# A two-layer graph network on one core: a direct tile's five products stand two picks behind its own pick on TensorE, and not one

## The reference

```
h = relu(layernorm(x));  x = x + segment_sum((h * cj)[src], dst) * ci
h = relu(layernorm(x));  x = x + (1 + eps) * h + segment_sum(relu(h[src] + edge_attr), dst)
```

## Time and profile before

| | |
|---|---|
| time, median of 3 runs | 4798.12 us (4794.34 to 4802.32) |
| the profiled execution | 4791.23 us, span 4789.2 us |
| layer 0's batches (first to last pick row L1157) | 200.74 to 3004.58 us of the span |
| PE busy | 3721.2 us (78%) |
| DVE busy | 3812.7 us (80%) |
| ACT busy | 3261.3 us (68%) |
| POOL busy | 3497.5 us (73%) |
| PE waited for ACT at L1259 (products) | 68.2 us |
| ACT waited for PE at L987 (copies) | 426.3 us |

### The profile page before, as it was taken

One profiled execution on the slowest core, in us unless ns is written; L12 is line 12 of the kernel. 1 busy time (PEld: TensorE's weight loads), 2 busy tenths in 40 slices (PEclk: granted clock), 3 DMA queues, 4 the chain that ended last, 5 costly groups with the idle time before them and its releaser, 6 DMA issues.

```text
span 4789.2 us, 130194 instructions
## 1 busy us (share of the span) xinstructions
PE 3721.2 (78%) x43852; PEld 2888.9 (60%) x43852; DVE 3812.7 (80%) x11454; ACT 3261.3 (68%) x9090; POOL 3497.5 (73%) x3590
## 2 busy tenths in 40 slices
PE   0388888888888888888888899467767777777775
PEld 0266666666666666666666666356666666666664
DVE  9788888888888888888888886767777776777775
ACT  1377777777777777777777777456666766666664
POOL 6757777777777777777777777477777777777774
PEclk9999999999999999999999999778888888888887
DMA  6322222222222222222222221211212221211221
GB/s 111 63 51 54 57 54 54 54 56 54 54 54 56 54 53 54 56 54 53 54 56 54 53 54 44 72 39 54 57 43 54 57 57 54 58 49 48 57 57 26
DMA packets 439702, 262.77 MB, mean 55 GB/s; under 512 B 334660, under 2 KB 423732, under 8 KB 432632
## 3 DMA queue, kind: packets, MB, share of 16 engines
q1 hardware_dynamic: 322488, 187.55, 16.7%
q0 software_dynamic: 110816, 60.69, 6.7%
q10 hardware_dynamic: 5728, 5.82, 0.5%
HBM read 172.96 MB, written 80.85 MB: 53 GB/s over the span
## 4 chain that ended last, share of the span: by engine, by line
PE 32%; POOL 23%; DVE 19%; issue 13%; ACT 10%; DMA 2%; DVEq 1%; ACTq 0%; SPq 0%; POOLq 0%
POOL stage L759 22%; PE candidates L1247 18%; PE plain_ps L1259 7%; DVE arena L1753 7%; ACT message L987 5%; DVE arena L1729 4%; ACT centered L956 2%; PE sorted_agg L1187 2%; PE candidates L1157 1%; ACT arena L880 1%; POOL message L759 1%; PE key_rows L1230 1%; DMA stage<-in_edge_attr 1%; DVE counts L1475 1%; PE key_rows L1139 1%
## 5 line engine op out<-in xcount | busy, mean ns | idle before, releaser
L771 POOL DMA_INDIRECT records<-stage,place_i x1875 | 1879.0, 1002 | 696.2 <-issue 652.0
L759 POOL DMA_INDIRECT stage<-table,src_plain x1250 | 1246.9, 997 | 409.1 <-issue 377.3
L987 ACT ACTIVATE message<-candidates,member_is 128x96 bf16<-128x96 f32 x4560 | 1170.7, 377 | 429.4 <-PE candidates L1247 426.3
L1753 DVE TENSOR_SCALAR arena<-window_iota,dst_rel 128x224 bf16<-128x224 f16 (+1 forms) x4800 | 1091.2, 302 | 37.8
L880 ACT ACTIVATE arena<-key_rows 125x640 f16<-125x640 f16 x1000 | 653.2, 716 | 215.1 <-DVE arena L1729 83.2
L1187 PE MATMUL sorted_agg<-arena 128*96 128x224 bf16 (+1 forms) x5000 | 654.1, 285 | 161.0 <-DVE arena L1753 109.6
L1259 PE MATMUL plain_ps<-summed,message 128*96 128x224 bf16 x4560 | 609.2, 269 | 68.2 <-ACT message L987 68.2
L1187 PEld LDWEIGHTS sorted_agg<-arena 128*96 128x96 bf16 x5000 | 543.7, 137 | 186.1 <-issue 118.6
L1259 PEld LDWEIGHTS plain_ps<-summed,message 128*96 128x96 bf16 x4560 | 490.7, 128 | 269.6 <-ACT message L987 127.4
L1729 DVE TENSOR_SCALAR arena<-arena,row_key 125x1280 bf16<-125x1280 f16 x1000 | 554.7, 555 | 96.5 <-ACT arena L880 64.6
L1139 PE MATMUL key_rows<-ident,record 128*125 128x128 f16 x5000 | 425.8, 235 | 239.2 <-DMA record<-records 96.2
(11 more groups left out here) (228 smaller groups left out, 5139.0 us busy)
## 6 DMA issues: line engine op xcount, KB each, us to landing
record<-records SPq DMA_DIRECT2D x50, 1650.0 KB
stage<-in_edge_attr SPq DMA_DIRECT2D x125, 400.0 KB, 3.2
records<-pad SPq DMA_DIRECT2D x25, 1650.0 KB, 11.9
records<-stage,place_i POOLq DMA_INDIRECT x1875
stage<-table,src_plain POOLq DMA_INDIRECT x1250
message<-table,mid_src POOLq DMA_INDIRECT x288
xs<-in_x SPq DMA_DIRECT2D x8, 390.6 KB
table<-parts ACTq DMA_DIRECT2D x4, 585.9 KB
```

The source lines that it names most:

```text
L759: pool.indirect_dma_start(message[:, k, j, :] if l == 0 else rows[:, k, j, :], None, table0 if l == 0 else table1, bass.IndirectOffsetOnAx ...
L771: pool.indirect_dma_start(records, bass.IndirectOffsetOnAxis(ap=place_i[:, h, e:e + 1], axis=0), stage[:, h, e, :], None).then_inc(scatter ...
L987: last = nc.scalar.activation(direct_message[n % DB][:, m * WIDE:(m + 1) * WIDE], candidates[n % 2][:, m * WIDE:(m + 1) * WIDE], ACT.Copy, ...
L1753: last = nc.vector.tensor_scalar(dst_onehot(g, t), window_iota[:, 0:WA if tile == 0 else WT], dst_rel[:, h, tile:tile + 1], None, ALU.is_e ...
```

## The change

In the loop over the direct tiles, the products of tile n - 2 stand behind the pick of tile n, where those of tile n - 1 stood. The range moves with them, so that tiles 0 to 33 are still done in the loop and tiles 34 to 37 behind it.

```
-                            if 1 <= n <= DIRECTS - LATE:
-                                direct_products(b, n - 1)
+                            if 2 <= n <= DIRECTS - LATE + 1:
+                                direct_products(b, n - 2)
```

## The result

| | time, median | ratio to before, 95% interval |
|---|---|---|
| before, 5 runs beside those of after | 4802.32 us (4794.34 to 4806.27) | |
| after, 5 runs | 4820.59 us (4815.02 to 4825.13) | 1.0036 [1.0025, 1.0047] |

The change makes the kernel 0.36% slower, 18.3 us between the medians; the interval of the ratio is 12 to 23 us. The forecast was 4818, 19.8 us of it for the change. The profiled execution took 4815.02 us, its span is 4812.9. Layer 0 ends 16.3 us later than in the profile of before (the first gather of layer 1 stood at 3112.2 and stands at 3128.5). The two spans differ by 23.7 us; the other 7.4 lie in layer 1, where nothing was changed. From its first gather on, layer 1 takes 1677 to 1695 us in the fourteen profiles of this case, and before's is the shortest, so these 7.4 us are a spread of executions and not the change's.

A forecast was written before the change was run, and what follows sets the result against it. ScalarE bounds seven direct tiles, then TensorE; VectorE's ranking runs full. Terms 1.05 + 1.62 + 14.58 + 2.58 give 19.8 us, on the median 4798.1: 4818 us; likeliest 4809 to 4822, 8-in-10 range 4794 to 4832.

The forecast's parts named there:

- The waits for ScalarE: First direct tiles: TensorE's waits for ScalarE's copies move to picks, sum staying near 68 us; TensorE's path 0.
- The first rival: First direct tiles: TensorE's 68.2 us of waits for ScalarE go, kernel takes 4730 us; chance 0.04.
- The one-hot of tile 27: VectorE, step 5: it waits for products of tile 16 and starts 1.62 us later in batches 1 to 21.
- From DVE to the pick: Batch end: 1.62 us reaches the pick in full in six batches VectorE ends, 1.29 in 15 ScalarE ends.
- The second rival: VectorE's lateness is hidden before the next batch's one-hots: up to 5 us faster, 4793 us; chance 0.17.
- Odd batches: Stops behind odd batches' products, tied to SyncE's fill, shrink 1.0 to 1.3 us; a pair costs 1.62, nine pairs 14.58.
- the third rival: Odd batches' stops don't shrink, all lateness is passed on: 30.1 us, 4828 us; chance 0.17, with or without the clock.
- TensorE's clock: The 20 products in five fast batches might slow by 1.54 us each, 7.7 in all; taken as 0, 4 in range.
- batch 22: Near the end, VectorE's 1.54 us wait for a later pick takes nearly all the lateness: 0.
- batch 0: First batch, where VectorE had no such wait for products of tile 16 before: 1.05 us later.
- batches 20 and 21: Last pair counted, without a stop behind the odd batch's products: 2.58 us later together.
- the gain from the earlier picks: Direct phase: picks up to 35 end 0.48 us earlier; worth 0.33 us in 15 batches, at most 5.0 us.

The follow-up runs named there:

- the run of the early tiles: Kernel before, with only the products of the first tiles, where TensorE waits for ScalarE, moved back a pick: 4797.77 us, ratio 1.0004.
- the late rank by itself: Kernel before, order and ring kept, with two more VectorE operations at the head of each batch's ranking: 4825.24 us, ratio 1.0042.
- with the fill moved: SyncE's fill issued only once the next batch's keys are turned: 4791.36 us in before's order, 4813.04 in the changed; with 13 ring places 4785.04 and 4771.67.
- before's order with 10 places: Kernel before, order of products kept, with 10 places in the ring of direct one-hots instead of 11: 4837.58 us, ratio 1.0077.
- With 13 places: Ring of direct one-hots given 13 places instead of 11: changed order 4792.16 us (0.9977 of before), before's order 4803.42 us (1.0005).

## Why the prediction was right, step by step

**The waits for ScalarE.** Forecast: they keep about their sum and stand before picks. They did (74.9 us, 144), and ACT's copies of tiles 6 and 7 stood at the same distance to 0.06 us. The first rival falls with the run of the early tiles: waits moved, time the same.

**The one-hot of tile 27.** +1.62 us was forecast. In batch 11 the products of tile 16 start 1.65 us later, and the one-hot with them (39.67 us behind the phase's start, 38.02 before). The sum of DVE's waits was put at some 60 us and is 73.0: besides tile 27's, each of batches 1 to 21 has the wait of tile 26, which I named and did not size in full.

**From DVE to the pick.** The rank was forecast at 78.3 and is at 77.9 to 78.6 in batches 1 to 21 (79.8 to 80.3 in batches 2, 6, 10, 14 and 18, whose rank came late before, too), 1.48 us later in the mean where 1.62 was forecast; the pick's wait was forecast at 3.7 us for DVE in all batches, and is 3.68 to 5.89, for DVE, in batches 0 to 21. POOL's scatter in batch 10 began 81.30 us behind the phase's start and 79.66 before. The second rival, lateness hidden, falls with this and with the late rank by itself.

**Odd batches.** The forecast was 1.62 for a pair and it is 1.40 in the profile, nearer than two profiles can tell. The stops did shrink, by 12.2 us together, 1.35 each; 1.0 to 1.3 was forecast. But the reason was half of the truth. One sign that I had named failed: the stops end 13.1 to 14.6 us behind the fill and not 12.3 to 13.5, so their end no longer hangs on the fill alone. A stop is TensorE's branch back to the loop's start, which I hadn't looked for; the fill lengthens it, and with the fill moved it keeps 3.3 to 4.0 us. Here the stops had just enough above that floor, which is luck: nothing in the prediction said how far they could shrink. With a little more lateness they can't, and before's order with 10 places, expected at 26 us, cost 36. On the Trainium skill, "Runtime: NRT & Kernel Launch", section "Instruction fetch mechanics": its "mostly hidden" is said of crossing from one block of instructions to the next. These nine stops are taken branches, and of those the same section says that a target outside the current two pages has to be fetched before execution can go on. The traces agree with that: 3.3 to 7.8 us with a transfer of instructions in each of the nine, and 0.08 us in batch 21, where the branch isn't taken. So the page didn't speak for the third rival, as I had it.

**TensorE's clock.** Taken at 0, with 4 us in the range. None of batches 1 to 21 does the 20 products in 2.08 us now; in the five where they did (1, 3, 4, 8 and 17) they take 3.0 to 3.7. The window behind batch 11's pick (columns as in the earlier trace rows), and one in batch 22; under them batch 22's in the kernel before:

```profile
1609.50:1613.50 4.00, 3.05 (x21) 2.82 (x19) 3.86 (x16) 0.92 (x2) 3.09 (x4) 0.73 0.49 101
2908.00:2911.00 3.00, 3.00 (x47) 3.00 (x44) 2.86 (x14) 1.75 (x4) 2.09 (x4) 1.00 0.08 17
2890.00:2895.00 5.00, 4.74 (x38) 4.77 (x39) 4.75 (x21) 1.30 (x3) 3.92 (x4) 0.50 0.08 17
```

At 0.73 part of the stretch ran at 1.2 GHz; the engine had stood 4.37 us before. In the odd batches with a stop (3 and 17) that costs nothing, as the floor shows: fast products only make the stop longer. Batches 1, 4 and 8 have no such stop, and their products take 3.9 us longer together. In batch 22 it went the other way: behind a wait of 2.43 us in both kernels the pick took 1.55 us, start to start, and the 20 products 3.94 before, at a granted clock of 0.50 (1.2 GHz), and they take 0.85 and 2.08 now, at 1.00. The batch is 3.3 us shorter, 1.0 us of it ahead of the pick. I had put both at 0, and that they partly cancel is luck. In which batches the products run fast differs from kernel to kernel here.

**The sum.** 19.8 us forecast, 18.3 measured between the medians (12 to 23 by the interval), 17.1 in the profile up to the start of batch 20. By term the profile has 0.23 us for batch 0 (1.05 forecast), 2.39 for batch 1 (1.62), 12.64 for the nine pairs (14.58), 0.77 for batches 20 and 21 (2.58) and -3.3 for batch 22 (0). Another 1.86 stand ahead of batch 0's direct phase and belong to no term; that start moves by as much between kernels without a cause in their edits. The direction and the pairs, three quarters of the sum, are the mechanism's. That the total came within 2 us is in part luck.

**A bound that was too narrow.** Ahead of the result I put the gain from the earlier picks at 5.0 us at most, since ACT's last copies would run into DVE's one-hots 0.33 us later. I had seen that DVE, too, comes 0.48 us earlier to tile 26, and left it out of that bound. With 13 places both engines are early and the order is worth 11.3 us, or 13.4 with the fill moved. The changed kernel had that gain in it, and its loss from the ring alone is about 28 us, not 18 (4820.59 against 4792.16, not measured side by side).

## What to carry to other kernels

When a consumer is moved back in a rotation of buffers, count the buffers less the steps of lateness. Here each step later needed one more place, and the same edit was 18 us slower with 11 places and about 10 us faster with 13. A wait for an engine that is full moves to the next instruction that needs it, so look instead at what else the moved instructions free: a one-hot of 0.28 us that waited 1.8 us held back the ranking of the batch two ahead. And a lateness that is swallowed by a stop is only lent: ask how far the stop can shrink, and what it is. Where the profile says "issue", look at the sequencer's own rows by the line of the loop: here they named a branch that no busy time shows.

## What the runs showed of the hardware

TensorE's branch back to the start of the loop of layer 0 (L501) took 3.3 to 7.8 us, nine times in each of fourteen profiles, and 0.08 us where the loop ended and it wasn't taken. ScalarE's branch at the same line took 0.04 to 0.06 us in the kernel before. In layer 1 TensorE's takes 4.0 to 5.2 us there, again nine times. In each of layer 0's one 16 KB transfer of an "instruction" queue lies within the branch, 0.9 to 1.7 us long, and the branch ended 1.3 to 1.9 us behind it. Two parts add up. With a write of 1,650 KB issued 12.1 to 14.6 us before TensorE's next instruction the transfer began up to 5.3 us after the branch, and the idle gap was 0.7 to 6.2 us; with that write behind the gap it began after 0.9 to 1.6 us, and the gap was 0.2 to 2.5. In the latter case the gap ended 3.9 to 4.8 us behind the start of the 20 products before it, in before's and the changed order, at 2.08 us for the products as at 3.94. That the branch waits for this transfer is read from where it lies; no row ties the two by name.
